# Causal attention dealt by group number: exponents right behind the first group's maxima, four value passes, three operand slots

## The chip, the cores and the metric

The kernel runs on one core of one Trainium2 chip. Its time is the device time of one execution in microseconds. Three executions of the kernel before gave 1312.33, 1309.05 and 1312.41 us, median 1312.33.

## The reference, cut to what matters

The program is one transformer layer on 4 sequences of 1024 rows of 256. The attention part, with 16 heads of 16 columns each, is what the change touches:

```
c_kv  = x @ W_dkv.T
q_lat = q @ k_eff                       # per head
attn  = q_lat @ c_kv.T / sqrt(16)       # causal: keys after the row are masked
attn  = softmax(attn)
y     = (attn @ c_kv) @ v_eff
```

A layer norm stands ahead of it and one behind it, and then a mixture of 8 experts of 1024 hidden columns, two for each row, with norms of its own.

## The kernel before, in words

**Stages.** `project` computes queries, keys and values of all sequences and stores them in the scratch tensors `qs`, `ks` and `vs`. `attend` does the attention. `route` and `experts` do the rest. Beside its own work `attend` splits the experts' weights: a half of an expert's weights is fetched into `raw`, split by POOL (GpSimd) into a high and a low part, and stored in `ws`, one half for each group.

**Groups.** Attention runs over 16 groups (4 sequences, 4 groups of 4 heads each). A group's queries, keys and values lie in a slot (`slots["q"]`, `["k"]`, `["v"]`); there are `NSL` = 4 slots. `load_group` (L83 to L101) fills one by 15 DMAs: 12 of 128 KB for queries and keys in their high and low parts, 2 of rows of ones, and one of 272 KB for the values, the last of them. Group 0's load is issued by ACT (ScalarE) in the projection, group 1's by ACT at the start of `attend`, group 2's by SP there, and the others by SP from its loop (L554 to L563).

**Maxima.** For each row of a group the maximum of its scores is found first. This is cut into 38 *units* (`max_units`): PE (TensorE) multiplies queries and keys into one of `NBK` = 3 banks `ps_m`, up to 512 columns wide (L650; L645 and L654 add the mask), and DVE (VectorE) reduces the bank (L797 to L805). When all units of a group are done, three small reductions form the negated maxima (`negate`), PE transposes them (a *turn*, L663), ACT copies them to `mt` (L745), and SP writes them by four small DMAs into spare rows of the query slot (`max_rows`, L521). With these rows in the queries, the scores come out less their maximum. In steady state `negate` of a group stands among the first three units of the next.

**Exponents and values.** A group then has 12 *blocks*, (half of the rows, 128 keys), and 24 *steps*, two heads of a block each. In a step PE makes the scores into one of two `ps_s` (L687) and ACT takes the exponent into `pt` (L772), a ring of `NPT` = 4 blocks. POOL clears what lies beyond the diagonal in 8 of the blocks (L595). A *values pass* on PE multiplies finished blocks by the values (L704), with 17 columns of weights for each of 4 heads, side by side in the array. Blocks on the diagonal are 512, 384, 256 and 128 columns wide, the four others 512. After the last block of a half ACT copies the sums (`ot`, L750), PE turns them back (L669, "out"), ACT copies again (L758), and POOL divides (L585, L587).

**The order of the work.** Each engine's list is written out from the same plan. `first` holds all 38 units of group 0 and 18 of group 1 with group 0's turn between; all of this comes ahead of the first step. In each step PE does the scores, then the units that `DEALT` deals *early*, then in every fourth step (1, 5, 9, ..., 21) a values pass of two blocks, then the units dealt *late*. During group g the units of group g+1 from the 18th on are done, and then the first 18 of g+2. The out jobs stand at steps 7 and 15, the turn at 17. On SP (L554 to L563) a group is: wait until the values of the group before are done, load group g+3, wait for the turn of g+1 and write its rows, wait for POOL's split, store both parts in `ws` (L543, L544), wait until they have landed (L545), and fetch the next weights (L533, L536). POOL splits at step 8.

```
if k % 4 == 1:
    for blk in (k // 2 - 2, k // 2 - 1):
        if blk >= 0:
            values(b, g, blk)
        elif b + g > 0:
            values(b, g - 1, NB + blk)
```

Of the kernel before, what the change touches and what calls it, by code (L numbers as in the profile page):

```python
# [56 lines left out]
NSL = NG  # L57
# [14 lines left out]
LOADS = 16 * (2 * 6 + 3) // NSL  # L72
# [10 lines left out]
def load_group(sp, d, slots, b, g):  # L83

    slot = g % NSL
    loaded, qg, kg = slots["loaded"][slot], slots["q"][slot], slots["k"][slot]
    qs, ks = (d[n][bass.ds(b + g // NG, 1)].rearrange("o k c t -> (o k) c t") for n in ("qs", "ks"))
    heads = slice(g % NG * GH * HS, (g % NG + 1) * GH * HS)
# [10 lines left out]
    w = slice(g % NG * GH * VW, (g % NG + 1) * GH * VW)  # L99
    sp.dma_start(slots["v"][slot][:], d["vs"][bass.ds(b + g // NG, 1)].rearrange("o p k w -> (o p) k w")[:, :, w]  # L100
# [6 lines left out]
def project(nc, d, keep, slots):  # L107


    with ExitStack() as ctx:  # L110
# [47 lines left out]
        with nc.Block() as block:  # L158
# [124 lines left out]
            def _(act):  # L283
# [38 lines left out]
                load_group(act, d, slots, 0, 0)  # L322
# [58 lines left out]
NPT = 4  # L381
DIAG = [n for n, (c, j) in enumerate(BLOCKS) if j >= c * TC]

# [28 lines left out]
HALF = NU // 4 * 2  # L412
NBK = 3
LOWEST = -3.0e38


def unit_keys(m):
# [28 lines left out]

def attend(nc, d, keep, slots):
# [3 lines left out]
    with ExitStack() as ctx:  # L451
# [29 lines left out]


        def at(b, g, per, more):
            return b * (NG * per) + (g * per + more)

        def ahead(b, g, n):

            return not isinstance(b, int) or b * NG + g + n < B * NG


        first = [("unit", 0, m) for m in range(NU)] + [("unit", 1, m) for m in range(HALF)]
        first[NU + 6:NU + 6] = [("turn", 0, 0), ("turn", 0, 1)]

        def numbered(b):


            out, n = [], len(first)
            for g in range(NG):
                steps = []
                for k in range(NS):  # L500
                    early, late = ([j for j in part if ahead(b, g, j[1])] for part in AFTER[k])
                    steps.append(Step((j, n + i) for i, j in enumerate(early + late)))
                    steps[-1].early = len(early)
                    n += len(steps[-1])
                out.append(steps)
            return out, n

        def turns(b, n):

            return b * (JOBS * NG // NBK) + n // NBK  # L510

        with nc.Block() as block:
            @block.sync
            def _(sp):
                def max_rows(g, b, n):

                    sp.wait_ge(bank_read[n % NBK], turns(b, n) + 1)
# [6 lines left out]
                def turn_job(steps):  # L524
                    return next(n for step in steps for what, n in step if what == ("turn", 1, 0))


# [11 lines left out]
                def keep_split(b, g):  # L539
# [6 lines left out]
                    if ahead(b, g, 1):  # L546
                        fetch_raw(b * (NG // 2) + (g + 1) // 2, (g + 1) % 2)
# [1102 lines left out]
```

## Time and profile before

| | us |
|---|---|
| median of three runs | 1312.33 |
| the profiled execution | 1311.21 |
| its span, first to last instruction | 1309.6 |
| PE busy | 1065.6 |
| DVE busy | 815.3 |
| ACT busy | 640.7 |
| POOL busy | 585.0 |

The profiled execution is 1.6 us longer than its span and 1.1 us below the median. Projection ends near 100, attention near 656, and the experts take the rest. Slots, semaphores and lists belong to attention alone, so only the stretch from 100 to 656 is edited. In the rows below PE is the matmul, PEld the weight load, `SPq` and `ACTq` the issue of a DMA by these engines; brackets at a row's end say how long the engine was idle ahead of it and what ended that.

### The profile page before, as it was taken

What the parts mean: (1) busy time and instruction counts of PE and PEld (TensorE: products, weight loads), DVE (VectorE), ACT (ScalarE), POOL (GpSimd) and SP (SyncE); (2) the same over time, 40 slices, a digit from 0 to 9 for tenths busy, and PEclk for the clock granted to TensorE, in tenths of its full rate; (3) what the DMA queues carried; (4) which work ended last, traced back from release to release, by engine and by line L of the source; (5) the groups of instructions that cost most, each with busy time, mean ns of one, the idle gap of its engine ahead of it and who ended that gap; (6) DMA issues with size and microseconds to landing.
All of it is one profiled execution on the core that took longest, in us unless ns stands there. A gap on an engine that the chain in (4) does not pass through costs nothing. (4 is left out here: it accounts for less than half of the span.)

```text
span 1309.6 us, 24611 instructions
## 1 busy us (share of the span) xinstructions
PE 1065.6 (81%) x7457; PEld 813.6 (62%) x7457; DVE 815.3 (62%) x2300; ACT 640.7 (49%) x1111; POOL 585.0 (45%) x675
## 2 busy tenths in 40 slices
PE   5966799999999999999805430999999999999900
PEld 2533455555555555555305330999999999999900
DVE  5737577777777777776068630555565556655567
ACT  2640266666666666666726420444444444444533
POOL 4204156556556565556646773122322222222237
PEclk9986699999999999999955555999999999999955
DMA  4998657777777777632444133414433414231173
GB/s 141 374 293 151 100 136 160 160 158 159 162 159 160 160 160 158 151 103 98 163 134 165 69 127 108 165 58 163 178 108 117 169 52 181 99 122 41 49 265 128
DMA packets 94609, 190.00 MB, mean 145 GB/s; under 512 B 28244, under 2 KB 59364, under 8 KB 86276
## 3 DMA queue, kind: packets, MB, share of 16 engines
q1 hardware_dynamic: 83584, 163.19, 44.9%
q0 software_dynamic: 7680, 22.09, 4.9%
q10 hardware_dynamic: 3272, 3.84, 2.2%
q8 instruction: 35, 0.57, 0.2%
q14 instruction: 38, 0.31, 0.1%
HBM read 109.54 MB, written 79.02 MB: 144 GB/s over the span
## 5 line engine op out<-in xcount | busy, mean ns | idle before, releaser
L772 ACT ACTIVATE att_pt<-att_ps_s 128x1024 f32<-128x1024 f32 (+3 forms) x384 | 297.8, 815 | 186.1 <-PE att_ps_s L687 181.0
L1512 ACT ACTIVATE moe_hf<-moe_ps_h,moe_b 128x256 f32<-128x256 f32 x288 | 134.5, 474 | 225.8 <-PE moe_ps_h L1468 211.5
L797 DVE CUSTOM_DVE_ANT_0 att_ps_m<-att_ps_m,keep_future 128x384 f32<-128x384 f32 (+1 forms) x256 | 153.9, 650 | 82.9 <-PE att_ps_m L650 82.9
L650 PE MATMUL att_ps_m<-att_k,att_q 128*128 128x512 f32 (+3 forms) x576 | 183.4, 391 | 1.2 <-DVE att_pm L797 0.6
L805 DVE TENSOR_REDUCE att_pm<-att_ps_m 128x1 f32<-128x512 f32 x256 | 161.4, 684 | 22.2 <-PE att_ps_m L650 22.2
L595 POOL TENSOR_SCALAR_AFFINE_SELECT att_pt<-att_pt 128x512 f32<-128x512 f32 x128 | 81.3, 636 | 200.0 <-ACT att_pt L772 200.0
L687 PE MATMUL att_ps_s<-att_q,att_k 128*128 128x512 f32 (+3 forms) x576 | 160.2, 367 | 6.3 <-ACT att_pt L772 5.2
L1421 POOL DMA_INDIRECT ys<-moe_o,moe_home x72 | 74.1, 1029 | 185.2 <-DVE moe_o L1551 172.3
L687 PEld LDWEIGHTS att_ps_s<-att_q,att_k 128*128 128x128 f32 x576 | 93.7, 189 | 60.9 <-issue 28.9
L1545 DVE TENSOR_TENSOR moe_hTl<-moe_hf,moe_hTh 128x256 fp32r<-128x256 f32 x288 | 124.0, 431 | 9.9
L650 PEld LDWEIGHTS att_ps_m<-att_k,att_q 128*128 128x128 f32 x576 | 104.7, 197 | 36.8 <-issue 11.9
L585 POOL TENSOR_TENSOR att_rec<-att_sums,att_minus 128x16 f32<-128x16 f32 x33 | 95.9, 2906 | 38.1 <-ACT att_sums L758 38.1
L704 PE MATMUL att_ps_o<-att_pt,att_v 128*17 128x512 f32 (+3 forms) x1152 | 107.1, 488 | 3.7 <-ACTq L740 3.1
L1543 DVE CAST moe_hTh<-moe_hf 128x256 fp32r<-128x256 f32 x288 | 84.3, 293 | 32.2 <-ACT moe_hf L1512 30.4
L1551 DVE TENSOR_TENSOR moe_o<-moe_ps_o,moe_b 128x256 f32<-128x256 f32 x72 | 27.2, 420 | 110.0 <-PE moe_ps_o L1479 110.0
L1468 PE MATMUL moe_ps_h<-moe_xTh,weights_w_0h 128*128 128x256 f32 x288 | 82.1, 285 | 5.4 <-issue 5.4
L1479 PE MATMUL moe_ps_o<-moe_w2h,moe_hTh 128*128 128x256 f32 x288 | 82.0, 285 | 0.0
L1479 PE MATMUL moe_ps_o<-weights_w_0h,moe_hTh 128*128 128x256 f32 x288 | 82.0, 285 | 0.0
L1468 PE MATMUL moe_ps_h<-moe_xTl,weights_w_0h 128*128 128x256 f32 x288 | 81.9, 284 | 0.0
L1468 PE MATMUL moe_ps_h<-moe_xTh,weights_w_0l 128*128 128x256 f32 x288 | 81.8, 284 | 0.0
L1468 PE MATMUL moe_ps_h<-moe_xTh,moe_w1l 128*128 128x256 f32 x288 | 80.9, 281 | 0.0
L1468 PE MATMUL moe_ps_h<-moe_xTl,moe_w1h 128*128 128x256 f32 x288 | 80.9, 281 | 0.0
(200 smaller groups left out, 2570.2 us busy)
## 6 DMA issues: line engine op xcount, KB each, us to landing
att_raw<-in_w SPq DMA_DIRECT2D x16, 1024.0 KB, 6.2
ws<-att_raw_hi SPq DMA_DIRECT2D x16, 1024.0 KB, 3.9
ws<-att_raw SPq DMA_DIRECT2D x16, 1024.0 KB, 5.8
moe_rows<-xs SPq DMA_DIRECT2D x38, 258.0 KB
att_q<-qs SPq DMA_DIRECT2D x66, 128.0 KB
att_k<-ks SPq DMA_DIRECT2D x66, 128.0 KB
weights_w_0h<-ws SPq DMA_DIRECT2D x8, 1024.0 KB
weights_w_0l<-ws SPq DMA_DIRECT2D x8, 1024.0 KB
```

Source lines behind the costliest of these rows:

```text
L585: pool.tensor_tensor(rec[:, c], got[:, :, :, HS], minus[:], ALU.pow).then_inc(rec_done, 1)
L650: ins = pe.matmul(out[:, end - keys:end], qg[slot][:, h // 2, i * P:(i + 1) * P], kg[slot][:, h, k0:k0 + keys], start=not whole, stop=not ...
L687: ins = pe.matmul(out[:, e, off:CH], kg[slot][:, 2 * p + e, j * P:(j + 1) * P], qg[slot][:, p, c * CH + off:(c + 1) * CH], start=True, sto ...
L704: ins = pe.matmul(ps_o[32 * h:32 * h + VW, off:CH], vg[slot][:, j, h * VW:(h + 1) * VW], pt[:, blk % NPT, h, off:CH], start=(j == 0), stop ...
L772: act.activation(pt[:, blk % NPT, 2 * p:2 * p + 2, off:CH], ps_s[k % 2][:, :, off:CH], ACT.Exp, scale=HS ** -0.5).then_inc(ex_done, 1)
L797: return dve.tensor_tensor_reduce(src, src, future[:, CH - keys:CH], 1.0, LOWEST, ALU.add, ALU.max, pm[:, g % 2, 0, h, place:place + 1])
L805: return dve.tensor_reduce(pm[:, g % 2, 0, h, place:place + 1], src, AX.X, ALU.max)
L1468: ins = pe.matmul(ps_h[f % NHB][:], w1[r][a][:, k, f * P:(f + 1) * P], xT[m][:, k], start=(n == 0), stop=(n == 3 * CT - 1))
L1479: ins = pe.matmul(ps_o[t][:], hT[a][:, f, t * P:(t + 1) * P], w2[r][m][:, f], start=(f == 0 and (a, m) == pieces[0]), stop=(f == FT - 1 an ...
L1512: act.activation(hf[:, f % NHB], ps_h[f % NHB][:], ACT.Relu, bias=b1[r][:, f:f + 1]).then_inc(hf_done, 1)
L1543: dve.tensor_copy(hT[0][:, f], hf[:, f % NHB]).then_inc(hh_done, 1)
L1545: dve.tensor_tensor(hT[1][:, f], hf[:, f % NHB], hT[0][:, f], ALU.subtract).then_inc(hl_done, 1)
```

## The change

- `NSL` goes from 4 to 3. SP loads group g+2 during group g instead of g+3, behind a wait that all values of group g-1 are done. Group 2's load is issued once group 0's rows are written and group 1's load has landed. The fourth slot's memsets go.
- The list ahead of the first step holds only group 0's 38 units and its turn. Group 0's first 8 steps have no units, its last 16 have 48 (`DEALT_FIRST`, of groups 1 and 2), group 1 has 44 (`DEALT_SECOND`, up to the 16th of group 3), and the later ones 38 by the new `DEALT`: 22 of g+1 and 16 of g+2. The last two groups have 22 and none.
- Values passes stand at steps 1 (four blocks, all of the group before), 9 (four), 13 and 17 (two each), and `NPT` goes from 4 to 6.
- The turn stands at step 16 (20 in group 0) as one job. Before it was two, the second empty.
- Counts of semaphores are written by group number, and the nops that raised some of them at the start go. SP's loop is written out.

The core of the diff; in `clear`, `values` and the exponents the place in `pt` is now `(g * NB + blk) % NPT`:

```diff
-NSL = NG
+NSL = 3
...
-LOADS = 16 * (2 * 6 + 3) // NSL
+LOADS = 16 * (2 * 6 + 3)
...
-def load_group(sp, d, slots, b, g):
-
-    slot = g % NSL
+def load_group(sp, d, slots, group):
+
+    b, g, slot = group // NG, group % NG, group % NSL
     loaded, qg, kg = slots["loaded"][slot], slots["q"][slot], slots["k"][slot]
-    qs, ks = (d[n][bass.ds(b + g // NG, 1)].rearrange("o k c t -> (o k) c t") for n in ("qs", "ks"))
-    heads = slice(g % NG * GH * HS, (g % NG + 1) * GH * HS)
+    qs, ks = (d[n][b] for n in ("qs", "ks"))
+    heads = slice(g * GH * HS, (g + 1) * GH * HS)
...
-NPT = 4
+NPT = 6
 DIAG = [n for n, (c, j) in enumerate(BLOCKS) if j >= c * TC]
+PASSES = {1: (-4, -3, -2, -1), 9: (0, 1, 2, 3), 13: (4, 5), 17: (6, 7)}
...
-HALF = NU // 4 * 2
+AHEAD = 16
+DEALT = ((1, 0), (1, 3), (1, 0), (1, 0), (1, 0), (2, 0), (2, 0), (1, 0), (1, 0), (1, 3), (1, 0), (1, 0),
+         (1, 0), (1, 2), (1, 0), (1, 0), (1, 0), (1, 2), (2, 0), (1, 0), (1, 0), (2, 0), (1, 0), (1, 0))
+DEALT_FIRST = ((0, 0),) * 8 + ((3, 0), (3, 3), (3, 0), (3, 0), (3, 0), (3, 3), (3, 0), (3, 0),
+                               (3, 0), (3, 3), (2, 0), (1, 0), (2, 0), (2, 0), (1, 0), (1, 0))
+DEALT_SECOND = ((2, 0), (1, 3), (2, 0), (2, 0), (2, 0), (2, 0), (2, 0), (1, 0), (1, 0), (1, 3), (2, 0), (2, 0),
+                (2, 0), (1, 2), (1, 0), (1, 0), (1, 0), (1, 2), (2, 0), (1, 0), (1, 0), (2, 0), (1, 0), (1, 0))
+OUT_STEPS = (7, 15)
...
-DEALT = ((1, 0), (1, 2), (1, 0), (2, 0), (2, 0), (1, 0), (2, 0), (0, 0), (2, 0), (1, 3), (1, 0), (2, 0),
-         (2, 0), (2, 0), (0, 0), (2, 0), (2, 0), (1, 0), (1, 0), (1, 0), (2, 0), (1, 1), (0, 0), (2, 0))
-assert sum(map(sum, DEALT)) == NU
-
-
-def bank_jobs():
-
-    work = iter([("unit", 1, m) for m in range(HALF, NU)] + [("unit", 2, m) for m in range(HALF)])
-    out = []
-    for k, (early, late) in enumerate(DEALT):
-        extra = {7: [("out", 0, 0)], 15: [("out", 0, 1)], 17: [("turn", 1, 0), ("turn", 1, 1)]}.get(k, [])
-        out.append((list(islice(work, early)) + extra, list(islice(work, late))))
-    return out
-
-
-class Step(list):
-
-    early = 0
-
-
-AFTER = bank_jobs()
-JOBS = sum(len(x) + len(y) for x, y in AFTER)
-assert JOBS % NBK == 0 and NB % NPT == 0
+class Step:
+
+
+    def __init__(self):
+        self.early, self.late = [], []
+
+    def all(self):
+        return self.early + self.late
+
+
+def all_jobs():
+
+
+    first = [(("unit", 0, m), m) for m in range(NU)] + [(("turn", 0, 0), NU)]
+    number = len(first)
+    units = [("unit", g, m) for g in range(1, GROUPS) for m in range(NU)]
+    groups = []
+    for g in range(GROUPS):
+        steps = []
+        for k, (early, late) in enumerate((DEALT_FIRST, DEALT_SECOND)[g] if g < 2 else DEALT):
+            step = Step()
+            steps.append(step)
+            for jobs, count in ((step.early, early), (step.late, late)):
+                for _ in range(count):
+                    if units and units[0][1] <= g + 2 and not (units[0][1] == g + 2 and units[0][2] >= AHEAD):
+                        jobs.append((units.pop(0), number))
+                        number += 1
+                if jobs is step.early:
+                    more = [("out", g, c) for c in range(2) if k == OUT_STEPS[c] and g + c > 0]
+                    more += [("turn", g + 1, 0)] if k == (20 if g == 0 else 16) and g + 1 < GROUPS else []
+                    for job in more:
+                        jobs.append((job, number))
+                        number += 1
+        groups.append(steps)
+    assert not units
+    return first, groups, (("out", GROUPS, 0), number)
+
+
+GROUPS = B * NG
+FIRST, DEAL, LAST = all_jobs()
+NUMBER = {job: n for job, n in [*FIRST, *(j for steps in DEAL for step in steps for j in step.all())]}
 
 
 def attend(nc, d, keep, slots):
...
+        def made(n):
+
+            return bank_made[n % NBK], n // NBK + 1
+
+        def read(n):
+
+            return bank_read[n % NBK], n // NBK + 1
+
+        def group_in(g):
+
+            return loaded[g % NSL], ONES + (g // NSL + 1) * LOADS
+
+        def rows_in(g):
+
+            return m_in[g % NSL], (g // NSL + 1) * 64
...
                 sp.wait_ge(slots["init"][2], 2)
                 load_ones(sp, d, slots, 2)
-                load_group(sp, d, slots, 0, 2)
-                def fetch_raw(expert, which):
-                    if which == 0:
-                        sp.dma_start(raw[:].rearrange("p (k f) -> p k f", k=CT),
-                                     d["w1"][bass.ds(expert, 1)].rearrange("o (k p) f -> (o p) k f", p=P)).then_inc(raw_in, 16)
-                    else:
-                        sp.dma_start(raw[:].rearrange("p (k c) -> p k c", c=C),
-                                     d["w2"][bass.ds(expert, 1)].rearrange("o (k p) c -> (o p) k c", p=P)).then_inc(raw_in, 16)
-
-                def keep_split(b, g):
-
-                    sp.wait_ge(split_lo, at(b, g, 2, 2))
-                    halves = d["ws"][bass.ds(b * (NG // 2) + g // 2, 1), g % 2]
-                    sp.dma_start(halves[0, 0], raw_hi[:].bitcast(F32)).then_inc(split_out, 16)
-                    sp.dma_start(halves[0, 1], raw[:]).then_inc(split_out, 16)
-                    sp.wait_ge(split_out, at(b, g, 32, 32))
-                    if ahead(b, g, 1):
-                        fetch_raw(b * (NG // 2) + (g + 1) // 2, (g + 1) % 2)
-
                 for u in range(2):
                     sp.wait_ge(keep["stored"][u], STORES * B + 1)
-                max_rows(0, 0, first.index(("turn", 0, 0)))
-                sp.wait_ge(slots["init"][3], 2)
-                load_ones(sp, d, slots, 3)
-                fetch_raw(0, 0)
-                def body(b):
-                    for g, steps in enumerate(numbered(b)[0]):
-                        if ahead(b, g, 3):
-
-                            sp.wait_ge(pv_done, at(b, g, NB, NPT))
-                            load_group(sp, d, slots, b, g + 3)
-                        if ahead(b, g, 1):
-                            max_rows(g + 1, b, turn_job(steps))
-                        keep_split(b, g)
-
-                with sp.Fori(0, B - 1) as b:
-                    body(b)
-                body(B - 1)
+                max_rows(0)
+
+                sp.wait_ge(*group_in(1))
+                load_group(sp, d, slots, 2)
+                fetch_raw(0)
+                for g in range(GROUPS):
+                    if 0 < g < GROUPS - 2:
+
+                        sp.wait_ge(pv_done, g * NB)
+                        load_group(sp, d, slots, g + 2)
+                    if g + 1 < GROUPS:
+                        max_rows(g + 1)
+                    keep_split(g)
...
+                def values_pass(g, k):
+                    for blk in PASSES[k]:
+                        if blk >= 0:
+                            values(g, blk)
+                        elif g > 0:
+                            values(g - 1, NB + blk)
+
+                pe.wait_ge(started, 1)
+
+                pe.matmul(ps_o[:], onesb[:, 0:P], onesb[:], start=True, stop=True)
+                jobs(FIRST)
+                for g, steps in enumerate(DEAL):
+                    for k, step in enumerate(steps):
+                        scores(g, k)
+                        jobs(step.early)
+                        if k in PASSES:
+                            values_pass(g, k)
+                        jobs(step.late)
+                values_pass(GROUPS, 1)
+                jobs([LAST])
...
+                fill_mt(0, NUMBER["turn", 0, 0])
+                for g, steps in enumerate(DEAL):
+                    for k, (c, j, p) in enumerate(STEPS):
+                        blk = g * NB + k // 2
+                        act.wait_ge(st_made, g * NS + k + 1)
+                        if blk >= NPT:
+
+                            act.wait_ge(pv_done, blk - NPT + 1)
+                        off = max(0, (j - c * TC) * P)
+                        act.activation(pt[:, blk % NPT, 2 * p:2 * p + 2, off:CH], ps_s[k % 2][:, :, off:CH],
+                                       ACT.Exp, scale=HS ** -0.5).then_inc(ex_done, 1)
+                        if k == 2 and g > 0:
+                            keep_out(g, 0)
+                        if k == 10:
+                            keep_out(g, 1)
+                        for what, n in steps[k].all():
+                            if what[0] == "turn":
+                                fill_mt(what[1], n)
+                            if what[0] == "out":
+                                keep_sums(g, what[2], n)
+                keep_out(GROUPS, 0)
+                keep_sums(GROUPS, 0, LAST[1])
```

## Rows read from the trace of the kernel before

**Rows 1.** The page, part 1: busy time, share of the span, instructions.
```profile
PE 1065.6 (81%) x7457; PEld 813.6 (62%) x7457; DVE 815.3 (62%) x2300; ACT 640.7 (49%) x1111; POOL 585.0 (45%) x675
```

**Rows 2.** Windows by stage; columns as in the first line.
```profile
core 0: us, PE busy (x) PEld busy (x) DVE busy (x) ACT busy (x) POOL busy (x), PEclk, DMA share, GB/s
97.90:100.70 2.80, 0.37 (x2) 0.00 (x0) 0.70 (x2) 0.80 (x3) 0.52 (x3) 1.00 1.04 404
100.70:124.90 24.20, 21.98 (x59) 11.23 (x59) 22.72 (x54) 0.00 (x0) 15.64 (x7) 0.70 0.82 131
124.90:139.40 14.50, 0.03 (x2) 0.06 (x2) 0.00 (x0) 0.00 (x0) 0.00 (x0) 0.50 0.95 110
139.40:152.40 13.00, 12.31 (x34) 7.75 (x35) 10.25 (x28) 0.27 (x1) 0.00 (x0) 0.50 0.14 44
152.40:184.40 32.00, 31.38 (x196) 19.24 (x195) 23.84 (x58) 20.06 (x29) 18.09 (x15) 0.96 0.64 119
216.20:248.00 31.80, 31.24 (x212) 18.69 (x212) 23.86 (x58) 20.05 (x30) 18.71 (x16) 1.00 0.77 160
627.17:655.70 28.53, 23.83 (x172) 10.99 (x172) 0.00 (x0) 20.19 (x30) 19.25 (x17) 1.00 0.40 153
```

**Rows 3.** Timelines of PE and ACT ahead of the first exponents: start, duration, engine.
```profile
139.37 0.58 PE L645 MATMUL att_ps_m<-keep_future,keep_identb 128*128 128x512 bf16 x1 [15.58 <-DMA att_v<-vs]
...
145.02 0.27 ACT L745 ACTIVATE att_mt<-att_ps_m 64x128 fp32r<-64x128 f32 x1 [46.05 <-PE att_ps_m L663]
```

**Rows 4.** Timeline of PE in one steady group.
```profile
303.47 0.27 PE L663 MATMUL att_ps_m<-keep_ident,att_pm 128*64 128x128 f32 x1
...
311.15 0.68 PE L650 MATMUL att_ps_m<-att_k,att_q 128*128 128x512 f32 x2
311.66 0.69 PE L687 MATMUL att_ps_s<-att_q,att_k 128*128 128x512 f32 x2
...
313.21 0.85 PE L704 MATMUL att_ps_o<-att_pt,slots_v 128*17 128x256 f32 x16
...
313.98 0.38 PE L650 MATMUL att_ps_m<-att_k,att_q 128*128 128x256 f32 x1
...
318.28 1.70 PE L704 MATMUL att_ps_o<-att_pt,att_v 128*17 128x512 f32 x16
319.91 0.44 PE L687 MATMUL att_ps_s<-att_q,att_k 128*128 128x128 f32 x2
...
326.32 0.39 PE L645 MATMUL att_ps_m<-keep_future,keep_identb 128*128 128x512 bf16 x1
...
326.94 0.68 PE L687 MATMUL att_ps_s<-att_q,att_k 128*128 128x512 f32 x2
...
327.46 0.39 PE L645 MATMUL att_ps_m<-keep_future,keep_identb 128*128 128x512 bf16 x1
...
329.85 1.91 PE L704 MATMUL att_ps_o<-att_pt,att_v 128*17 128x512 f32 x16
331.69 1.20 PE L687 MATMUL att_ps_s<-att_q,att_k 128*128 128x512 f32 x4
```

**Rows 5.** Timeline of SP's DMA issues in the same group.
```profile
304.83 2.65 SPq L521 DMA_DIRECT2D att_q<-att_mt  x4
307.78 0.38 SPq L543 DMA_DIRECT2D ws<-att_raw_hi  x1
...
314.26 0.41 SPq L536 DMA_DIRECT2D att_raw<-in_w  x1
314.94 0.37 SPq L95 DMA_DIRECT2D slots_q<-qs  x1
```

**Rows 6.** Short windows of the DMA engines in two steady groups, columns as in Rows 2.
```profile
320.00:322.00 2.00, 2.00 (x14) 1.80 (x15) 1.14 (x4) 1.27 (x4) 0.58 (x1) 1.00 0.99 123
334.00:336.00 2.00, 1.70 (x12) 1.02 (x14) 1.76 (x7) 2.00 (x4) 1.23 (x1) 1.00 0.02 3
267.40:269.40 2.00, 2.00 (x14) 1.17 (x7) 0.00 (x0) 0.58 (x1) 1.24 (x1) 1.00 0.80 104
```

More of the change, by code:

```diff
@@ L2 @@
 from contextlib import ExitStack
-from itertools import islice
 import numpy as np
@@ L480, in attend @@
         pm_done, nh_hi, nh_done = (s.sem(n) for n in ("pm_done", "nh_hi", "nh_done"))
[L483 to L510, printed above, removed]
+        def made(n):
[6 more added lines that the diff above has]
+            return m_in[g % NSL], (g // NSL + 1) * 64
         with nc.Block() as block:
@@ L522, in max_rows, with fetch_raw @@
                                      mt[h * 2 * TB:(h + 1) * 2 * TB, :].bitcast(F32)).then_inc(m_in[slot], 16)
-                def turn_job(steps):
-                    return next(n for step in steps for what, n in step if what == ("turn", 1, 0))
+                def fetch_raw(n):
+                    if n % 2 == 0:
+                        sp.dma_start(raw[:].rearrange("p (k f) -> p k f", k=CT),
+                                     d["w1"][n // 2].rearrange("(k p) f -> p k f", p=P)).then_inc(raw_in, 16)
+                    else:
+                        sp.dma_start(raw[:].rearrange("p (k c) -> p k c", c=C),
+                                     d["w2"][n // 2].rearrange("(k p) c -> p k c", p=P)).then_inc(raw_in, 16)
@@ L605, in split, with unit @@
                         part = slice(n * HALF_W // 2, (n + 1) * HALF_W // 2)
[L606 removed]
+                        pool.wait_ge(split_hi, 2 * g + n + 1)
                         pool.tensor_tensor(raw[:, part].bitcast(F32R), raw[:, part], raw_hi[:, part], ALU.subtract
                                            ).then_inc(split_lo, 1)
[L610 to L621 removed]
+                for g, steps in enumerate(DEAL):
+                    for k, step in enumerate(steps):
+                        if k == TB:
+                            split(g)
+                        if k % 2 == 1 and k // 2 in DIAG:
+                            clear(g, k // 2)
+                        for what, n in step.all():
+                            if what[0] == "out":
+                                divide(g, what[2], n)
+                divide(GROUPS, 0, LAST[1])
             @block.tensor
             def _(pe):
[L625 to L635 removed]
+                def unit(g, m, out):
                     heads, pieces = UNITS[m]
@@ L704, in values @@
                         ins = pe.matmul(ps_o[32 * h:32 * h + VW, off:CH], vg[slot][:, j, h * VW:(h + 1) * VW],
[L705 removed]
+                                        pt[:, (g * NB + blk) % NPT, h, off:CH], start=(j == 0), stop=(j == (c + 1) * TC - 1))
                     ins.then_inc(pv_done, 1)
[L708 to L721 removed]
@@ L723, in _ @@
-                for b in range(B):
-                    body(b)
-                for blk in (NB - 2, NB - 1):
-                    values(B - 1, NG - 1, blk)
-                jobs(B - 1, NG, [(("out", 0, 0), numbered(B - 1)[1])])
+                def values_pass(g, k):
[5 more added lines that the diff above has]
+                pe.wait_ge(started, 1)
@@ L784, in _ @@
-                for b in range(B):
-                    body(b)
-                keep_out(B, 0, 0)
-                keep_sums(B - 1, NG, 0, numbered(B - 1)[1])
+                fill_mt(0, NUMBER["turn", 0, 0])
+                for g, steps in enumerate(DEAL):
+                    for k, (c, j, p) in enumerate(STEPS):
[13 more added lines that the diff above has]
+                                fill_mt(what[1], n)
+                            if what[0] == "out":
+                                keep_sums(g, what[2], n)
```

206 lines of the change are left out of this document (75 added, 131 removed).

## The prediction

> **What bounds the kernel now.** I read the page first: TensorE (PE) is busy 81% of the span [rows 1]. Then a table of stages cut at the groups' first scores [rows 2]. After the projection come 38 units of maxima of group 0 (100.7 to 124.9), a hole of 14.5 us in which no engine works, 18 units of group 1, and group 0's exponents from 152.4. The hole ends when PE gets group 1's operands: it waited 15.58 us for the DMA of `att_v`, the last transfer of a load [rows 3]. From 184.4 a group takes 31.8 us, with PE busy 31.2 of it, VectorE (DVE) 23.9 and ScalarE (ACT) 20.1: PE bounds it. The last group has no units and takes 28.5 us to the end of attention at 655.7, bounded by ACT and PE in turn. What follows attention is not edited.
>
> Next I followed one steady group on PE, from its first scores at 311.66 [rows 4], the issues of SP [rows 5], and the DMA engines' share in short windows [rows 6]. The reader is to see a chain: the maxima rows of the next group leave SP at 304.83, both stores of the split weights follow at 307.78, SP waits for them, fetches the next weights at 314.26 and only then issues the next group load at 314.94, 3.3 us into the group. The load then needs long: the share is 0.99 at 123 GB/s at 320 to 322 and falls to nothing only in 334 to 336. I put the landing at about 334, 22.4 us after the group's start. In the group that starts at 248.0 the share is down to 0.80 in 267.4 to 269.4, so it ends about 21 us in. I take 21.6 +- 0.8. Before, this is harmless: the load is for three groups on.
>
> **The change part by part.**
> (a) *Groups ahead.* With three slots the load issued in group g is that of g+2. Its first unit is the 23rd of group g's list (22 units of g+1 are left, as 16 were done ahead), so it stands right behind the values pass of step 13. When does PE get there? Before, that pass ends at 331.69, 20.0 us in, after 25 units and 8 value blocks [rows 4]. The new order has 3 units fewer: the five first units of the next group leave (326.32 to 329.85 is 3.53 us, less two score steps of 0.52, as 326.94 to 327.46: 2.5 us), and two plain ones come (0.26 each, as from 311.15 to 311.66): -2.0. It has two blocks more, of 512 and 384 columns: 1.63 us, less two saved passes (b): +1.2. So PE is there 19.2 us in, and a little later where three banks of DVE's 0.6 us hold a unit up: 19.4. The load's start barely moves: the turn of the next maxima goes from step 17 to 16, but three more units and one values pass fewer stand behind it (+0.8 and a step of 0.8, against -1.63), so it stays about 8.2 us ahead of the group's end (303.47 to 311.66), and the rows, stores and weights that follow it on SP keep their times. The new wait for all earlier values is met near 3.9 us instead of 3.3, while the weights are still in flight. The DMA engines are full from then on, so the landing stays near 21.6. PE waits 21.6 - 19.4 = 2.2 us. Nothing covers it: PE runs in order, and behind the wait stand the units, then the scores, on which ACT, POOL and the next load depend. It recurs in groups 2 to 13: 12 x 2.2 = **+26.4 us**. Ends: 0.7 (the earliest landing, the latest need) and 3.4.
>
> The Trainium skill, "DMA: Bandwidth & Descriptors", Specifications, gives the fabric 435 GB/s; by that alone a load of 1.9 MB (12 of 128 KB, the values and the ones; an estimate: 4.3 us) would be in long before the 19th microsecond and the wait would be nil. The trace disagrees: the 123 GB/s of the load stand at a share of 0.99, so I go by the row.
>
> (b) *Four passes instead of six.* The pass of blocks with 256 and 128 columns takes 0.77 us to the next unit (313.21 to 313.98), that with 512 and 384 takes 1.63 (318.28 to 319.91): 512 more columns cost 0.86, or 1.68 ns each, so the 384 of the first are 0.64 and 0.13 is left for a pass by itself. What its entry adds no row shows alone; between 0 and 0.2 I take 0.07, nearer to 0 since PE is never idle ahead of a pass for more than that. Two passes of 0.2 us fewer give -0.4 us a group, bounds -0.26 and -0.66. Over groups 2 to 13: **-4.8 us**. A pass of four blocks keeps PE 2.3 us; ACT has two score buffers (20.1 us over 24 steps, 0.84 each) and DVE three banks of 0.6. Both then idle briefly, which costs nothing while PE is the bound. Six exponent buffers cover the longer distance.
>
> (c) *The start.* Group 0's 38 units end at 124.9 as before. Three small reductions, transpose and copy (0.27 us) [rows 3] take about 2 us; SP's four row transfers 2.65 us plus landing. Steadily the latter has at most 4.2 us (307.5 to 311.66, no wait seen); between 0 and 4.2 I take 1.1, since these 32 KB go when the queues are nearly idle. Group 0's scores start near 130.5 instead of 152.4. Eight steps without units are ACT's: 28% of the columns of a group, 28% of 20.1 = 5.6 us. Then 48 units in 16 steps: DVE needs 22.7 us for 38 in the first stage, 0.60 each, so 28.7, and PE about as much; together, not perfectly overlapped, 31 us. That ends near 167. The turn of group 1 stands at step 20, so its rows arrive 2 us late: group 1 at 169, before 184.4.
>
> (d) *Group 1.* 44 units, six more than 38: +1.8 us of PE. SP's chain starts late too: rows until 168.6, stores to 175, then weights and group 3's load, landing 19 us after the weights' issue (314.26 to 334 less the range), at 194. PE wants it 19.4 us in, at 188.5: a wait of 5.5 us. Group 1 takes 31.4 + 1.8 + 5.5 = 38.7 and group 2 starts at 207.8, before 216.2: **-8.4 us** for (c) and (d) together. Bounds -14 (rows in time, a shorter chain) and -3.
>
> (e) *The rest.* Group 14 has two units more (+0.6) and the saved passes; group 15 is ACT's and PE's in turn and loses perhaps half a microsecond of handovers: **-0.5**. The fourth slot's two memsets on POOL and SP's loop registers go: 0, as POOL has nothing to do then until the exponents, and SP waits for DMAs. If that cover were gone it would be some 5 us of POOL, once.
>
> Sum: -8.4 + 26.4 - 4.8 - 0.5 = +12.7. The profiled execution took 1311.2 us (its span 1309.6 and 1.6 around it), 1.1 under the median of the runs, 1312.3; so 1323.9 by it and **1325.0 us** as a median.
>
> **The rivals.**
> *The load lands in time* (faster). If it landed 2.2 us earlier, or the first 13 steps took 2 us longer at no cost elsewhere, the sum is -8.4 - 4.8 - 0.5 = -13.7, with group 1's wait gone too -19: 1293 to 1299. For it: the hole of 14.5 us is certainly filled, by work that PE can do. Against it: at 19.4 to 21.4 us of a group the share is still 0.80 (267.4 to 269.4) [rows 6]. It decides at a wait of 1.1 us a group, where the sum is nil. Between 0.8 and 1.5 us lies the case of no change, within 4 us or 0.3%, about what a measurement of this kernel can tell from none.
> *The passes were the point* (faster still). Should a switch into column tiles cost more than the rows show, 1 us each, two saved in each of 16 groups would give 32 us and outweigh the wait: 1325 less the 27 that is more than I count, about 1298. Against it: the two passes' rows leave 0.13 us. Little chance.
> *The waits halve the clock* (slower still). After the hole the granted clock was 0.50, the 1.2 GHz level, and stayed there through 13 us of PE work [rows 2]. If each new wait brought it down for some 5 us of matmuls, a third of the 13, that is 2.5 us more in 12 groups: 1355. Against it: from 97.9 to 100.7 PE was busy 0.37 us, and the clock stayed at 1.00 (it fell later, in the stage of units alone, to 0.70 of full speed in the mean); 2.2 us is nearer to that than to 14.5. Group 1's 5.5 us may do it once. The Trainium skill, "TensorE: Matmul & The Clock Gate", Part 1, has idleness bring the half-rate state back; by it alone every wait would be suspect.
> *The change does not do what it says.* The dealing leaves group 0 with 48 units where 54 are open to it, so part of the early start is only moved to group 1; that is in (c) and (d). Were it also late for the rows in group 1 and 2, a further 3 us each, the sum would be +19; that lies in the forecast's range.
>
> **How the numbers follow.** The wait of 2.2 us (1.5 to 3.4, sums +4 to +27): 0.59, forecast 1325, own range 1316 to 1339. The clock: 0.04. No change: 0.13. The load in time: 0.21, and the passes' case 0.03. The range takes in the upper bound of the wait and most of the faster side: 1297 to 1339, with the clock's case and the last of the faster ones left out. Faster 0.24, same 0.13, slower 0.63.
>
> **What would show it.** Group 0's first exponent near 131 and no hole at 124.9; group 2's first scores near 208; then groups of about 33.6 us, PE idle some 2 us each in front of the first maxima matmul (the masked one of 512 columns) with the DMA of `att_v` or `slots_v` as releaser; values in four stretches a group. A period of 31.3 us, or a DMA share that has fallen by the 19th microsecond, would prove (a) wrong; a first group longer than 40 us (c).

## The result: 3.3% slower, outside the range

The changed kernel took 1353.2 us in the median of four executions (1347.4 to 1363.4 us), the kernel before beside it 1312.1: a ratio of 1.033, 95% interval 1.027 to 1.039. The forecast was 1325, range 1297 to 1339; the direction was right, the size was not.

The page of the changed kernel's profiled execution (1357.6 us), part 1, to be set against [rows 1]:

```profile
span 1355.9 us, 24199 instructions
...
PE 1088.1 (80%) x7453; PEld 827.6 (61%) x7453; DVE 815.8 (60%) x2300; ACT 644.5 (48%) x1109; POOL 578.2 (43%) x671
```

PE has 22.5 us more of busy time with four matmuls fewer on record, which already says that some of its matmuls run slower. The windows cut at the groups' first exponents (columns as in [rows 2]), the first row group 0, the last group 15:

```profile
133.82:178.78 44.96, 40.37 (x200) 23.72 (x200) 29.30 (x73) 20.26 (x28) 15.30 (x14) 0.88 0.39 76
178.78:216.25 37.47, 35.56 (x218) 21.00 (x218) 27.34 (x65) 20.66 (x30) 18.40 (x16) 0.97 0.65 159
216.25:250.32 34.07, 31.82 (x212) 19.02 (x211) 23.64 (x57) 20.24 (x29) 18.90 (x17) 1.00 0.69 150
250.32:289.40 39.08, 34.60 (x212) 21.20 (x211) 24.04 (x58) 20.43 (x29) 18.76 (x17) 0.91 0.63 131
...
323.57:357.41 33.84, 31.80 (x212) 19.02 (x211) 23.95 (x58) 20.23 (x29) 18.77 (x17) 1.00 0.64 149
357.41:393.10 35.69, 31.81 (x212) 19.03 (x211) 23.96 (x58) 20.24 (x30) 18.76 (x17) 1.00 0.69 144
...
427.27:466.27 39.00, 34.98 (x212) 21.59 (x211) 24.03 (x58) 20.42 (x29) 18.77 (x17) 0.91 0.63 130
...
534.99:572.62 37.63, 33.34 (x212) 20.11 (x211) 23.95 (x58) 20.43 (x29) 18.78 (x17) 0.95 0.62 131
...
671.65:702.50 30.85, 25.82 (x186) 11.84 (x186) 0.00 (x0) 20.21 (x29) 19.20 (x17) 0.94 0.37 142
```

Group 2 starts at 216.3, where the kernel before has 216.9: the filled hole brought 0.7 us. Groups 2 to 13 take 425.3 us against 12 x 31.8 = 381.8: +43.5. The last two groups take about 4 us more, and what follows attention is unchanged. PE's timeline shows a wait for the next-but-one group's load in every one of the twelve, 20.8 us in all; four of them (start, duration, engine, as in [rows 3]):

```profile
273.88 0.59 PE L637 MATMUL att_ps_m<-keep_future,keep_identb 128*128 128x512 bf16 x1 [3.19 <-DMA att_v<-vs]
...
344.69 0.38 PE L637 MATMUL att_ps_m<-keep_future,keep_identb 128*128 128x512 bf16 x1 [0.74 <-DMA att_v<-vs]
...
380.38 0.38 PE L637 MATMUL att_ps_m<-keep_future,keep_identb 128*128 128x512 bf16 x1 [2.60 <-DMA att_v<-vs]
...
450.38 0.40 PE L637 MATMUL att_ps_m<-keep_future,keep_identb 128*128 128x512 bf16 x1 [2.72 <-DMA att_v<-vs]
```

Take each wait off its group's length: 34.17 - 1.11, 33.84 - 0.74, 35.69 - 2.60, 34.69 - 1.63 and 35.26 - 2.15 all give 33.1 us. Three groups leave more, 35.9, 36.3 and 34.7, and these are the ones with a granted clock under 1.00. So the 43.5 us are three things: load waits, 20.8 us; a group that takes 33.07 us without its wait, not 31.8 (12 x 1.27 = 15.2); and the clock, 2.8 + 3.2 + 1.6 = 7.6. Short windows around the wait of 3.19 us show the last; the first row is the wait, the others the matmuls behind it:

```profile
270.70:273.90 3.20, 0.02 (x1) 0.05 (x2) 0.00 (x0) 0.00 (x0) 0.48 (x1) 0.88 0.30 49
273.90:275.90 2.00, 2.00 (x9) 1.81 (x10) 0.65 (x2) 0.00 (x0) 0.00 (x0) 0.50 0.00 0
275.90:277.90 2.00, 2.00 (x9) 1.50 (x9) 0.92 (x4) 0.49 (x1) 0.00 (x0) 0.50 0.00 0
277.90:279.90 2.00, 2.00 (x9) 1.50 (x9) 0.82 (x2) 1.26 (x2) 0.00 (x0) 0.50 0.00 0
279.90:281.90 2.00, 2.00 (x16) 1.49 (x18) 1.36 (x4) 1.67 (x4) 0.95 (x1) 0.99 0.00 0
```

Six microseconds at the 1.2 GHz level, with 9 matmuls in 2 us instead of about 16. Behind the wait of 2.60 us the clock stayed:

```profile
377.80:380.40 2.60, 0.02 (x1) 0.06 (x2) 0.00 (x0) 0.00 (x0) 0.46 (x1) 1.00 0.53 64
380.40:382.40 2.00, 2.00 (x15) 1.74 (x15) 1.22 (x3) 0.07 (x1) 0.00 (x0) 1.00 0.03 8
```

### The profile page after: what moved, and what is told of

The parts are those of the page before. It is cut to its first block and busy times, and to the rows that moved or that the text cites. A ratio compares the mean times of both kernels' runs of the same rounds, so it can differ in the third digit from the quotient of the medians.

```text
span 1355.9 us, 24199 instructions
## 1 busy us (share of the span) xinstructions
PE 1088.1 (80%) x7453; PEld 827.6 (61%) x7453; DVE 815.8 (60%) x2300; ACT 644.5 (48%) x1109; POOL 578.2 (43%) x671
## 5 line engine op out<-in xcount | busy, mean ns | idle before, releaser
L642 PE MATMUL att_ps_m<-att_k,att_q 128*128 128x512 f32 (+2 forms) x480 | 165.1, 401 | 2.9 <-DVE att_pm L787 1.3
L679 PE MATMUL att_ps_s<-att_q,att_k 128*128 128x512 f32 (+1 forms) x480 | 138.4, 371 | 13.0 <-ACT att_pt L757 9.3
L589 POOL TENSOR_TENSOR att_rec<-att_sums,att_minus 128x16 f32<-128x16 f32 x32 | 93.1, 2908 | 102.2 <-ACT att_sums L746 102.2
L642 PEld LDWEIGHTS att_ps_m<-att_k,att_q 128*128 128x128 f32 x480 | 89.6, 201 | 43.6 <-issue 12.5
L679 PEld LDWEIGHTS att_ps_s<-att_q,att_k 128*128 128x128 f32 x480 | 82.6, 193 | 37.7 <-ACT att_pt L757 28.2
L642 PE MATMUL att_ps_m<-slots_k,slots_q 128*128 128x512 f32 (+3 forms) x288 | 102.9, 429 | 0.9 <-DVE att_pm L787 0.5
L679 PE MATMUL att_ps_s<-slots_q,slots_k 128*128 128x512 f32 (+3 forms) x288 | 85.6, 386 | 13.3 <-ACT att_pt L757 8.3
L696 PE MATMUL att_ps_o<-att_pt,att_v 128*17 128x512 f32 (+1 forms) x960 | 85.2, 488 | 0.0
```

Source lines behind the costliest of these rows:

```text
L589: pool.tensor_tensor(rec[:, c], got[:, :, :, HS], minus[:], ALU.pow).then_inc(rec_done, 1)
L642: ins = pe.matmul(out[:, end - keys:end], qg[slot][:, h // 2, i * P:(i + 1) * P], kg[slot][:, h, k0:k0 + keys], start=not whole, stop=not ...
L679: ins = pe.matmul(out[:, e, off:CH], kg[slot][:, 2 * p + e, j * P:(j + 1) * P], qg[slot][:, p, c * CH + off:(c + 1) * CH], start=True, sto ...
L696: ins = pe.matmul(ps_o[32 * h:32 * h + VW, off:CH], vg[slot][:, j, h * VW:(h + 1) * VW], pt[:, (g * NB + blk) % NPT, h, off:CH], start=(j ...
```

## The experiments

Theory A: the landing of the load sets the period, and the waits take the clock with them. Rivals: the passes of four blocks (B), and the new dealing (C). "Before" is measured beside each run, with medians of 1310 to 1312 us.

**Keep PE busy in the wait (e_warm).**

```diff
                     if m == 0:
+                        for _ in range(8 if g > 2 else 0):
+                            pe.matmul(out[:], identb[:], future[:], start=True, stop=True)
                         pe.wait_ge(*group_in(g))
```

> The changed kernel with eight 512-column bf16 multiplications of PE put ahead of each load wait from group 3 on (about 1.8 us, into the bank that the unit overwrites), so that most of the wait is no idleness. Clock theory (the 2.6 to 3.2 us waits let the granted clock fall, which costs 4 to 5 us in each group where it happens): no group of 39 us is left, groups take 34 to 35.5 us, the clock is 1.00 from group 2 to 13, the median falls from 1353 to 1340 or less. Rival, that the 39 us groups come from something else (a late transfer, POOL): they stay, and the filling adds up to 1 us in groups that wait little, median 1353 to 1365.

Measured: 1360.1 us, ratio 1.036 [1.034, 1.038]. The mechanism showed: the clock is 1.00 in all of groups 2 to 13 and none takes 39 us. The total missed: PE comes to the load 21.0 us into a quiet group of the changed kernel (344.69 - 0.74 - 322.91, where the group's scores start), and 8 fillers carry it past the landing in eight of the twelve groups (in the others 0.25 to 0.93 us of waiting is left), so that each group pays for them. A group takes 34.7 us and more where the changed kernel's quiet group takes 33.8:

```profile
283.40:318.12 34.72, 33.26 (x222) 19.74 (x224) 23.97 (x57) 20.23 (x30) 18.74 (x17) 1.00 0.68 147
```

**Take the load's rival for the DMA engines away (e_noraw).** This kernel leaves out 15 of the 16 weight fetches, so its outputs past attention are computed from the wrong weights.

```diff
-                    if n + 1 < GROUPS:
-                        fetch_raw(n + 1)
...
-                    pool.wait_ge(raw_in, 16 * g + 16)
+                    pool.wait_ge(raw_in, 16)
+                    if g > 0:
+                        pool.wait_ge(split_out, 32 * g)
```

> The changed kernel, but SP fetches the experts' weights only once; POOL splits what lies there and the stores stay. It leaves out 15 fetches of 1 MB. Landing theory (a group lasts from its start to the landing of the load, 21.7 us, and 12.0 more): the load lands 3 to 4 us earlier, no load wait is left, and the period is set by the other engines' holds in the first 13 steps, 21.0 + 12.0 = 33.0 us; the clock stays at 1.00; about 1330. Rival, that the four passes and the new dealing cost nothing by themselves: 31.4 us a group, about 1310.

Measured: 1328.3 us (a single run), no wait for a load but two of 0.16 us, clock 1.00, and every group from 2 on at 33.0 to 33.2 us. The group of 33.1 us is thus real without any load wait: still 1.3 us longer than before's 31.8.

**Remove the wait by need, not by landing (e_ahead12).** Twelve units ahead, maxima closed behind their own last unit, turn at step 17.

```diff
-AHEAD = 16
+AHEAD = 12
...
-                        if m < 3 and g > 1:
-                            negate(g - 1, m)
-                        if m == NU - 1 and g in (0, GROUPS - 1):
+                        if m == NU - 1:
```

> The changed kernel, but the maxima of a group are closed behind its own last unit, only 12 units of group g+2 are dealt in group g instead of 16, and the turn stands at step 17. The first unit of g+2 is then the 27th of the list, at step 16, 22 to 23 us into the group, behind the landing at 21.7. Landing theory: load waits under 0.7 us, no fall of the clock, groups of 32 to 33 us, 1318 to 1332. Rival (the passes and dealing make the period, whatever the load does): 33.7 us and more, 1340 or more.

Measured: 1332.4 us, ratio 1.016 [1.014, 1.017], no load wait after one of 0.47 us in group 1 and one of 0.60 us in group 2, clock 1.00, groups of 32.72 us:

```profile
291.57:324.29 32.72, 31.72 (x212) 19.03 (x211) 23.90 (x57) 20.05 (x30) 18.74 (x17) 1.00 0.73 156
```

Three slots are affordable, then, if the units ahead are fewer; but 0.9 us a group stays.

**Six passes in the changed kernel (e_six).**

```diff
-PASSES = {1: (-4, -3, -2, -1), 9: (0, 1, 2, 3), 13: (4, 5), 17: (6, 7)}
+PASSES = {1: (-2, -1), 5: (0, 1), 9: (2, 3), 13: (4, 5), 17: (6, 7), 21: (8, 9)}
```

> The changed kernel with the six passes of two blocks back at steps 1, 5, 9, 13, 17 and 21, everything else as changed (three slots, 16 ahead, ring of six). Landing theory: PE reaches the first unit of g+2 earlier, near 19.5 us, waits longer (2 to 3 us in most groups), and the period stays landing 21.7 + 12 us = 33.5 to 34, with a fall of the clock in as many groups or more: 1340 to 1375, no faster than the changed kernel by over 1%. Rival (the four passes are what costs): groups of 31.5 to 32 us, 1320 or less.

Measured: 1354.2 us, ratio 1.032 [1.028, 1.035], the changed kernel's own time. The waits are there again (3.52 us at 274.56, 1.24 at 311.91), and the clock falls in the group of the longer one. It also falls behind a wait of 2.09 us at 523.94, shorter than the 2.60 us above: the granted clock is 1.00 through that wait and 0.51 in the 2 us behind it. Groups that keep the full clock take 32.9 us without their wait:

```profile
252.46:292.05 39.59, 34.88 (x212) 21.08 (x211) 24.34 (x58) 20.42 (x29) 18.70 (x17) 0.91 0.65 129
292.05:326.24 34.19, 31.76 (x212) 18.50 (x211) 24.26 (x58) 20.25 (x30) 18.74 (x17) 1.00 0.69 150
```

**The order of before, three slots alone (e_slots).** Dealing, passes, ring and start of before; `NSL = 3`, group g+2 loaded in group g, 18 units ahead.

> The order of the kernel before (18 units ahead of the start, six passes, ring of four, its dealing, written by group number) with three slots, the load of g+2 in group g. Landing theory: the first unit of g+2 is the 21st, wanted 14 to 15 us into a group, so PE waits 7 us in every group, the clock falls in each, and a group lasts 21.7 + 17 to 21 = 38.5 to 43 us: 1390 to 1450. Rival (the load is faster when it is wanted sooner, or hidden): 32 to 35 us a group, under 1350.

Measured: 1435.4 us (a single run). Need comes early, the landing does not, and PE waits 7 to 9 us in every group:

```profile
359.62 0.59 PE L638 MATMUL att_ps_m<-keep_future,keep_identb 128*128 128x512 bf16 x1 [7.01 <-DMA att_v<-vs]
402.38 0.59 PE L638 MATMUL att_ps_m<-keep_future,keep_identb 128*128 128x512 bf16 x1 [8.85 <-DMA att_v<-vs]
```

The group of the first has a clock of 0.87 and 40.9 us. Theory A stands for the waits and the clock, from both sides; the 1.3 us of e_noraw it does not explain.

**The new start alone (e_start).** Everything of before in the steady groups (four slots, ring of 4, six passes, `DEALT`, turn at 17, 18 ahead) with the changed kernel's start and its single turn job.

> The kernel before in slots (four), ring (four), six passes, steady dealing and turn, with the new start alone: exponents right behind group 0's maxima, 8 steps without units, then 48, then 46 in group 1. Theory: the hole of 14.5 us is filled, group 0 takes 42 to 45 us (cold clock and DVE), groups from 2 on 31.8 us and no load waits; group 2 starts 3 to 9 us earlier than at 216.9; 1303 to 1310. Rival (the start gives all back in groups 0 and 1): 1310 to 1315, no difference.

Measured: 1301.5 us, ratio 0.992 [0.990, 0.994]. Group 2 starts at 212.3, and the groups take 31.25 us, not 31.8:

```profile
306.10:337.30 31.20, 30.98 (x212) 18.66 (x211) 23.80 (x58) 19.96 (x29) 18.65 (x17) 1.00 0.74 163
```

**The second, empty turn job back (e_two).** e_start with one nop more in the list of PE, and its wait and signal on ACT.

> The new start in the order before (run e_start, groups of 31.25 us) with the second, empty turn job back, as the kernel before has it: PE, ACT and the bank pass it on without work. Theory: ahead of the values pass of step 17 ACT must pass the empty bank on before PE can fill the next one; groups go back to 31.8 us, 14 groups x 0.55 = 8 us, 1309. Rival (the gain of e_start a group comes from somewhere else, as SP's loop or semaphore counts): 1301 to 1303 stays.

Measured: 1305.1 us, ratio 0.995 [0.993, 0.996], groups of 31.54 us. The empty job takes one of the three banks for a round and costs 0.29 us a group, half of what I expected: behind it PE waits 0.22 us for ACT ahead of the values pass (301.38), where e_start has no wait. The other 0.27 up to before's 31.8 was not looked into.

**Is it the passes? (e_a12_six).** e_ahead12 with six passes.

> Three slots as in e_ahead12 (12 units ahead, maxima closed behind their own last unit, turn at step 17), but six values passes of two blocks in place of four; the ring stays at 6. E_ahead12 had no load wait, a granted clock of 1.00 and groups of 32.72 us, against 31.25 in e_start with six passes and four slots. If the four-block passes make that difference (ACT out of score buffers, DVE out of banks), groups here are 31.3 to 31.8 us, ACT is busy through the stretch of a pass, and the time is 1315 to 1323. If it is the dealing or the closing of the maxima, groups stay at 32.5 to 32.9 and the time at 1330 to 1334. A third outcome: PE comes to the next-but-one group's first unit before its load is in, since nothing holds it up on the way; then waits of up to 1.5 us stand there again and groups are 31.8 to 33.

Measured: 1327.7 us, ratio 1.014 [1.012, 1.016]; the steady groups take 32.95 us, *more* than the 32.72 with four passes. B falls as the cause of the long groups: here the passes of four blocks save 0.24 us a group. In the changed kernel's own order, with 16 units ahead and the turn at step 16, they do not: there a group without its wait takes 33.07 us with four passes and 32.92 with six (e_six). The two profiled executions leave attention together all the same (the first matmul behind it at 696.0 and 695.9): group 1 has a load wait of 5.2 us here. The totals part behind attention, where neither kernel is edited.

**Is it the dealing? (e_start_deal).** e_start with the new `DEALT` and 16 ahead, nothing else.

```diff
-DEALT = ((1, 0), (1, 2), (1, 0), (2, 0), (2, 0), (1, 0), (2, 0), (0, 0), (2, 0), (1, 3), (1, 0), (2, 0),
-         (2, 0), (2, 0), (0, 0), (2, 0), (2, 0), (1, 0), (1, 0), (1, 0), (2, 0), (1, 1), (0, 0), (2, 0))
+DEALT = ((1, 0), (1, 3), (1, 0), (1, 0), (1, 0), (2, 0), (2, 0), (1, 0), (1, 0), (1, 3), (1, 0), (1, 0),
+         (1, 0), (1, 2), (1, 0), (1, 0), (1, 0), (1, 2), (2, 0), (1, 0), (1, 0), (2, 0), (1, 0), (1, 0))
```

> E_start (four slots, ring of 4, six values passes, turn at step 17; groups of 31.25 us, 1301.5 us) with one thing of the change added: the new dealing of units over the steps, and 16 units ahead in place of 18. No load can be late here, since group g+3 is loaded in group g. E_a12_six showed that six passes in place of four leave a group at 32.96 us, so the passes are not what a group of the changed kernel costs beyond its load wait. If it is the dealing (no step without a unit, clusters of four at steps 1 and 9, three at 13 and 17), groups are 32.6 to 33.1 us here and the time 1318 to 1325. If it is the three slots themselves, or the closing of the maxima behind their own last unit, groups stay at 31.2 to 31.5 and the time at 1301 to 1305.

Measured: 1319.5 us, ratio 1.007 [1.005, 1.009], every steady group 32.87 us. C is shown: with four slots, no load wait and a full clock, the dealing costs 1.6 us a group. (The two units fewer ahead go with it; their number is not the cause, by e_ahead12 above and e_a11_old below: 12 and 11 ahead, and otherwise only the dealing between them.) The groups by line say where; PE's scores in one group of this run:

```profile
L681 PE MATMUL att_ps_s<-slots_q,slots_k 128*128 128x512 f32 (+3 forms) x46 | 13.1, 365 | 1.1 <-ACT att_pt L759 0.9
```

and in one of e_start:

```profile
L681 PE MATMUL att_ps_s<-att_q,att_k 128*128 128x512 f32 (+3 forms) x49 | 13.5, 362 | 0.1
```

In the changed kernel's quiet group (323.57 to 357.41) the same 0.9 us stand:

```profile
L679 PE MATMUL att_ps_s<-att_q,att_k 128*128 128x512 f32 (+3 forms) x46 | 12.9, 362 | 1.1 <-ACT att_pt L757 0.9
```

0.9 us is PE waiting for ACT to empty a score buffer, in e_start_deal in two waits of 0.46 and 0.45 us, 5 and 16 us into the group. Both stand at the end of a run of three steps with one unit each (2 to 4, 10 to 12). Ahead of such a run are the pass and the late units of step 1 or 9, behind which ACT was itself idle for 1.25 and 1.06 us; then the short steps come faster than ACT empties its buffers. ACT's rows at the second run show it:

```profile
325.08 1.03 ACT L759 ACTIVATE att_pt<-att_ps_s 128x1024 f32<-128x1024 f32 x1 [1.06 <-PE att_ps_s L681]
326.01 0.59 ACT L739 ACTIVATE att_ot<-att_ps_o 128x512 f32<-128x512 f32 x1
```

PE starts the scores of these steps 0.8 and 0.9 us apart (324.41, 325.23, 326.16); ACT needs 1.0 us for the exponents of one, and at step 10, as at step 2, it also copies the sums of a finished half (0.59 us). Both runs have that copy at these steps, but only the new dealing puts it at the head of a run of short ones. PE's busy time is 0.7 us higher too, 31.7 against 31.0, on the same work. Why was not taken apart, so the mechanism is shown for 0.9 of the 1.6 us and not for the rest.

**Three slots with the dealing of before (e_a11_old).** The changed kernel with its four passes and ring of six, `DEALT` of before in groups 2 to 15, 11 ahead.

> The changed kernel with its three slots, ring of six and four passes, but the dealing of the kernel before in groups 2 to 15, 11 units ahead, maxima closed behind their own last unit, turn at step 17. If the dealing makes the 1.5 us between 32.72 (e_ahead12) and 31.25 (e_start), groups are 31.0 to 31.5 us: four passes save 0.24 us against six (32.72 against 32.96). Against e_ahead12 that is 14 groups by 1.5, so 1308 to 1315. PE then comes sooner to the first unit of the next-but-one group (the 28th, near step 16, some 22 us in, against a landing at 21.7), so a load wait of up to 0.7 us may stand in some groups, which gives up to 1320. If the four-block passes cost by themselves, groups are 32.3 or more and the time 1326 or more.

Measured: 1323.9 us, ratio 1.010 [1.008, 1.011]: above the forecast. The dealing gives its time back: the two groups without a wait take 31.74 us from turn to turn, 1.0 us less than in e_ahead12, and in the one from 441.47 PE has no wait for ACT. With it PE is early for the load again: from group 2 on ten waits of 0.6 to 2.3 us. One of them took the clock along although it, too, was shorter than the 2.60 us above; the wait and the two stretches behind it:

```profile
535.20:537.50 2.30, 0.03 (x2) 0.07 (x2) 0.86 (x5) 1.31 (x3) 1.83 (x1) 1.00 0.32 44
537.50:539.50 2.00, 2.00 (x9) 1.82 (x10) 0.67 (x1) 0.00 (x0) 1.69 (x2) 0.50 0.00 0
539.50:541.50 2.00, 2.00 (x14) 1.44 (x17) 0.76 (x3) 0.51 (x1) 0.00 (x0) 0.65 0.00 0
```

**A version that beats both (e_fill).** e_start with the hole filled on DVE as well: 9 units of group 1 ahead of the first step, the turn behind two of them, 47 more over all 24 steps of group 0, group 1 as any other.

```diff
-    first = [(("unit", 0, m), m) for m in range(NU)] + [(("turn", 0, 0), NU)]
+    first = [("unit", 0, m) for m in range(NU)] + [("unit", 1, m) for m in range(9)]
+    first[NU + 2:NU + 2] = [("turn", 0, 0)]
+    first = [(job, n) for n, job in enumerate(first)]
```

> The run e_start with 9 units of group 1 ahead of the first step (two before group 0's turn) and 47 more dealt over all 24 steps of group 0, so DVE works through the wait for the rows and through the first 8 steps, and group 1 has the steady dealing. Theory: group 0's 16 us without DVE work are what delays groups 1 and 2; group 2 starts near 200 instead of 212.3, 1287 to 1293. Rival (PE's cold clock, not DVE, holds group 0): group 2 starts at 207 or later, 1296 or more.

Measured: 1291.4 us, ratio 0.985 [0.982, 0.987], faster than both. Two things change at once, DVE's idle time and the clock, and no run separates them. The windows: between group 0's units and the rows, and group 0:

```profile
126.10:130.00 3.90, 2.77 (x17) 2.03 (x16) 3.50 (x12) 0.27 (x1) 0.00 (x0) 1.00 0.00 0
...
134.10:169.20 35.10, 34.30 (x201) 19.75 (x200) 28.20 (x68) 20.01 (x28) 15.23 (x14) 1.00 1.06 192
```

In the changed kernel the same stretch is nearly empty, and the first eight steps behind it run at the lower clock with DVE idle:

```profile
126.00:133.80 7.80, 1.63 (x4) 1.18 (x5) 1.52 (x7) 0.27 (x1) 0.00 (x0) 0.50 0.22 46
133.82:141.90 8.08, 7.47 (x22) 4.68 (x22) 0.00 (x0) 6.40 (x9) 2.56 (x4) 0.50 1.03 130
```

## Why the prediction was wrong, step by step

**(a) The load wait** was right in kind and place, and a little large: 20.8 us against 26.4, 1.7 a group against 2.2. That it came so near is in part luck, as two errors lean against each other. The need was at 21.0 us in every group, not 19.4: e_six, with two value blocks fewer ahead of it, has 19.3 where the forecast's terms give 18.2, so about 1.1 us is the new dealing and 0.5 the two blocks (an estimate from these numbers). And the load landed at 21.6 to 24.2 us, 22.8 in the mean, not at 21.6; six of the twelve lie beyond the forecast's 22.4. Its first transfer was issued 3.9 us in each time, as forecast, and the load landed 17.7 to 20.3 us later; why that varies was not looked into. The Trainium skill, "DMA: Bandwidth & Descriptors", Specifications, with its 435 GB/s would have had no wait; twelve waits speak against reading it that way for this load, whose transfers move 124 GB/s at a share of 1.13 in the changed kernel too:

```profile
339.00:341.00 2.00, 1.64 (x6) 0.67 (x4) 2.00 (x7) 2.00 (x4) 2.00 (x2) 1.00 1.13 124
```

**(b) The passes, and the sentence that failed.** The two passes fewer save 0.24 us a group by e_ahead12 and e_a12_six, just under my bound of 0.26, and nothing in the changed kernel's own order, where e_six has the shorter groups. What failed is that I priced the new dealing by its number of units alone, and let ACT and DVE "idle briefly, which costs nothing while PE is the bound". PE is the bound over a group, but not in every step: with two score buffers ACT bounds a run of steps that have one unit, and the time lost there isn't regained in a step with four: 0.9 us a group. Groups without their wait took 33.07 us, not 31.4: instead of -4.8 us this part made +15.2, 20 us of the 34 by which the profiled execution missed its forecast of 1323.9. Run by run, a group without its wait is 31.8 us before, 31.25 in e_start, 32.87 with the new dealing (e_start_deal), 32.92 with three slots, the ring of six and the turn at step 16 (e_six), and 33.07 with four passes (the changed kernel). The dealing is +1.6 of that (+1.0 between e_ahead12 and e_a11_old, with three slots and four passes), the new start and the single turn job give 0.56 back, and slots and passes together are +0.2. A slower need also shortens the wait, so the two terms are not independent, as e_a11_old shows.

**The clock.** The rival that I gave 0.04 came true in part: 3 of 12 groups at 1.6 to 3.2 us each, 7.6 us. My reason against it, one window with PE idle for 2.4 of 2.8 us at a clock of 1.00, was the row of a single case. The Trainium skill, "TensorE: Matmul & The Clock Gate", Part 1, has idleness bring the half rate; the trace agrees for waits of 2.72, 2.98 and 3.19 us and not for the one of 2.60 us, which left the clock at 1.00. The spread of the changed kernel's executions, 16 us where the kernel before has 3, fits a number of such groups that differs from one execution to the next; only profiled ones show it. The mean granted clock of the four whole executions goes the same way, from 0.893 in the fastest to 0.886 in the slowest.

**(c), (d) The start.** 0.7 us instead of 8.4. The first scores came at 132.6, not 130.5. PE's last unit of group 0 ended at 125.8, not 124.9; the 2.0 us that I had for reductions, transpose and copy went on the reductions alone, and the transpose took 0.4 more; PE then waited 4.35 us for the copy and the rows' DMA, where I had put 2.65 plus 1.1. The eight steps without units took 8.1 us, not 5.6, at a granted clock of 0.50, where it had stood through the mostly idle 7.8 us ahead of them; the 48 units behind took 34.6 us, not 31. Group 1's rows were then 2.3 us late, as forecast (2). Only its load wait was smaller, 1.2 us for 5.5. e_start has the same start with a group 0 of 44.2 us, and e_fill shows what was missing: with work for DVE and PE in the hole, and the clock at 1.00 from there on, group 0 takes 35.1 us with 47 of the units in it.

**(e) The tail**, the last two groups, was 4 us longer, not half a microsecond shorter: about 1 us in group 14, whose units are dealt the new way, and about 3 in group 15, with the clock at 0.94. There the clock fell behind a stretch with waits of only 0.54 and 0.69 us:

```profile
675.00:677.00 2.00, 0.90 (x5) 0.36 (x3) 0.00 (x0) 1.93 (x4) 0.00 (x0) 1.00 0.37 91
677.00:679.00 2.00, 1.62 (x11) 1.28 (x11) 0.00 (x0) 1.64 (x5) 1.28 (x2) 1.00 0.98 310
679.00:681.00 2.00, 2.00 (x10) 1.03 (x12) 0.00 (x0) 1.65 (x4) 1.76 (x2) 0.57 0.38 131
```

The two profiled executions differ by 46.4 us and the medians by 41: the changed kernel's profiled execution is one of its slower two.

## What to carry to other kernels

Price a dealing of work over steps step by step, against each engine's buffers: a bound that holds on average over a group says nothing of a step in which another engine holds the last buffer. When a buffer is taken away, compare the landing of its load with the need in the same group, and let the need come later (fewer units ahead) rather than accept a wait that recurs; and a hole is worth filling on every engine that has work for it, not only on the one that waits.

## What the runs showed of the hardware

- A wait's length alone did not decide whether the granted clock fell: not behind 2.60 us in the changed kernel, but behind 2.29 us in e_a11_old and 2.09 us in e_six, and behind a stretch with waits of 0.54 and 0.69 us in the last group.
- The load of a group, issued at the same place each time and of the same size, landed 17.7 to 20.3 us behind its first issue in the changed kernel.
- A fall lasted 6 us of full PE work behind the 3.19 us wait, and 2 to 4 us behind the 2.29 us one.
- A job of no work that only takes its turn in the round of three banks cost 0.29 us a group (31.54 against 31.25 us, e_two and e_start).
